# Cross attention on one core: other places in the queue for the large loads, key parts in transfers of 24 rows, split maxima sent one step earlier

## The chip, the cores and the metric

One core of a Trainium2 chip (trn2) runs one launch. The metric is the device time of that launch in microseconds (us), lower is better. Engines: PE (matmul), ACT (ScalarE), DVE (VectorE), POOL (GpSimd), SP (SyncE, which only issues DMAs). Matmuls run at a clock that the chip grants: 2.4 GHz (shown as 1.00) or 1.2 GHz (0.50).

## The reference, cut to what matters

Cross attention of 16 batch rows with 256 queries each over 1601 keys (16 heads of 8 dimensions), then a local-attention block of 6 layers that the change does not touch:

```
scores = einsum('bhqd,bhkd->bhqk', q, k) / sqrt(8)
scores = where(mask, -1e9, scores)
attn   = softmax(scores)                     # over 1601 keys, fp32
x      = x + tanh(g) * (einsum('bhqk,bhkd->bhqd', attn, v) @ w_o + b_o)
```

## The kernel before, in words

`cross_phase` handles one batch row per iteration, and three rows are in flight: `cur` (its softmax and its products), `nxt` (its keys, queries and values are projected, its operands loaded) and `prev` (its output). An iteration has 4 groups, q = 0 to 3, of 4 heads each, and a group has KT = 13 steps, one per tile of 128 keys. Below, "step (q, kt)" is step kt of group q.

In every step PE makes the scores of one key tile into the two banks `b_e` (line 756 adds the mask, line 760 multiplies keys and queries); ACT takes exp of each into `eT` (line 442, two instructions a step); PE multiplies the exps of the step before with the values (line 662). A bank of `b_e` is written again only when its exp of the step before is done, so PE and ACT hold each other to within one step. Beside that PE makes other scores `b_s` (line 742), two groups ahead, from which DVE takes the maxima (line 515), and the small matmuls of `nxt` and `prev` (the list in `uses`).

**Operands.** q and k are split into three bfloat16 parts. They go out to DRAM (`k_scr`, line 303; `q_scr`, line 313) and come back in another layout: `k_op[q]`, one tensor for each group, rows 24a + 8c + d (a, c = 0 to 2, d = 0 to 7) by `load_k` in nine transfers of 8 rows of 12808 bytes (line 265); `q_op`, for all groups, in nine transfers of 8 rows (line 322). The negated maximum of each query goes into three further rows of `q_op`: PE transposes it at step TURN = 7, DVE negates it (line 528), POOL splits it in three with five small instructions (`max_parts`, lines 363 to 372, semaphore `mp_ready`), and ACT sends the parts in three small transfers (line 486) at step 10 of the group before the one that reads them; PE waits for them (`mrow_in`) at step 0 of that group, ahead of line 756.

**Order on SP's queue in one iteration:** `xa`, `xb` (lines 284, 290), `x1_scr`, `xn_scr` (293, 296), `k_scr`, then `load_k` 0 (waits until group 0 of `cur` is done with `k_op[0]`), `q_scr`, `q_op` (waits for the last but one row only), `load_k` 1 (waits for group 1), the next row's context `ctxT` (line 255) and masks (258, 259), `load_k` 2 (group 2), `load_k` 3 (group 3). SP takes them strictly in turn.

**At step (0, 10)** ACT also makes a part of the keys (`kp`, line 461) ahead of the small transfers. At step (0, 7) it made the first one (line 457), on which POOL's subtraction (line 379) waits; `max_parts` is queued behind that.

Of the kernel before, what the change touches and what calls it, by code (L numbers as in the profile page):

```python
# [48 lines left out]
HX, DK = 16, 8  # L49
MROW = 9 * DK  # L50
KEYS = 1601
KT = -(-KEYS // P)
# [42 lines left out]
def cross_phase(nc, x1_scr, xn_scr, ident, identb, ins, NB):  # L95
# [6 lines left out]
    with ExitStack() as ctx:  # L102
        def sb(name, shape, dt=F32):
            return ctx.enter_context(nc.sbuf_tensor(name, shape, dt))

        def sem(name):
            return ctx.enter_context(nc.semaphore(name))
# [10 lines left out]
        k_op = [sb(f"k_op{i}", [P, 4, KEYS], BF16) for i in range(4)]  # L118
# [28 lines left out]
        k_scr = nc.dram_tensor("k_scr", [2, 3, P, KEYS], BF16, kind="Internal").ap()  # L147
# [21 lines left out]
        s = {n: sem(n) for n in (*per, *dma_per)}  # L169
        per.update(dma_per)  # L170
        kop_in = [sem(f"kop_in{i}") for i in range(4)]
        KOP = 9 * 16
        pool_passed = sem("pool_passed_x")
        dve_passed = sem("dve_passed_x")
        start_in = sem("start_in")
# [19 lines left out]
        def count(name, b, c, back=0):  # L195

            return (b - back + AHEAD) * per[name] + c

        def max_index(q):

            return 1 if q == 3 else q + 2

        def start_ahead(eng, names):
            for name in names:
                eng.sem_inc(s[name], AHEAD * per[name])
# [40 lines left out]
        @block.sync  # L246
        def _(sp):
            start_ahead(sp, dma_per)
            for dst, src in ((w_sb[:, :], ins["x_w"]), (vec[:, :], ins["x_vec"]), (bv[:, :], ins["bv"]),
                             ):  # L250
                sp.dma_start(dst, src).then_inc(start_in, 16)

            def load_ctx(b):

                sp.dma_start(ctxT[:, :], ins["ctx"][:, b, :]).then_inc(s["ctx_in"], 16)

            def load_masks(b):
                sp.dma_start(m8[:, :, :], ins["mask_q"][b]).then_inc(s["m8_in"], 16)
                sp.dma_start(mt8[:, :, :], ins["mask_k"][b]).then_inc(s["mt8_in"], 16)

            def load_k(b, p, q):
                for a in range(3):
                    for c in range(3):
                        r = 24 * a + 8 * c
                        sp.dma_start(k_op[q][r:r + DK, :, :],
                                     k_scr[p, c].rearrange("(d h) k -> d h k", d=DK)[:, 4 * q:4 * q + 4, :]
                                     ).then_inc(kop_in[q], 16)

            load_ctx(0)
            load_masks(0)
            sp.wait_ge(set_pool, N_SETX)
            for i in range(4):
                sp.dma_start(k_op[i][MROW:MROW + 3, :, :], onesr[:, :].unsqueeze(1).to_broadcast([3, 4, KEYS])
                             ).then_inc(ones_in, 16)

            def iteration(cur, nxt, prev, base):
                if nxt:
                    b = nxt[0]  # L280

                    sp.wait_ge(start_in, 48)
                    sp.wait_ge(s["lcq_ready"], count("lcq_ready", b, 1, back=1))
                    sp.dma_start(xa[:, :], ins["xin"][:, b, :]).then_inc(s["xa_in"], 16)
                if prev:
                    b = prev[0]

                    sp.wait_ge(start_in, 48)
                    sp.wait_ge(s["y1_ready"], count("y1_ready", b, 1, back=1))
                    sp.dma_start(xb[:, :], ins["xin"][:, b, :]).then_inc(s["xb_in"], 16)  # L290
                    sp.wait_ge(start_in, 48)
                    sp.wait_ge(s["y1_ready"], count("y1_ready", b, 1))
                    sp.dma_start(x1_scr[:, b, :], y1[:, :]).then_inc(s["x1_kept"], 16)
                    sp.wait_ge(start_in, 48)
                    sp.wait_ge(s["xn_ready"], count("xn_ready", b, 1))
                    sp.dma_start(xn_scr[:, b, :], xn[:, :]).then_inc(s["xn_kept"], 16)
                if nxt:
                    b, p = nxt
                    sp.wait_ge(start_in, 48)
                    sp.wait_ge(s["klo_ready"], count("klo_ready", b, 1))  # L300

                    for c in range(3):
                        sp.dma_start(k_scr[p, c], kp[:, c, :]).then_inc(s["kscr_in"], 16)
                    sp.wait_ge(start_in, 48)
                    sp.wait_ge(s["kscr_in"], count("kscr_in", b, 48))

                    sp.wait_ge(start_in, 48)
                    sp.wait_ge(s["e_done"], count("e_done", b, 2 * KT, back=1))
                    load_k(b, p, 0)
                    sp.wait_ge(start_in, 48)  # L310
                    sp.wait_ge(s["qlo_ready"], count("qlo_ready", b, 1))
                    for c in range(3):
                        sp.dma_start(q_scr[p, c], qp[:, c, :]).then_inc(s["qscr_in"], 16)
                    sp.wait_ge(start_in, 48)
                    sp.wait_ge(s["qscr_in"], count("qscr_in", b, 48))

                    sp.wait_ge(start_in, 48)
                    sp.wait_ge(s["e_done"], count("e_done", b, 8 * KT, back=2))
                    for a in range(3):
                        for c in range(3):  # L320
                            r = 24 * a + 8 * c
                            sp.dma_start(q_op[r:r + DK, p, :, :], q_scr[p, a].rearrange("(d h) q -> d h q", d=DK)
                                         ).then_inc(s["qop_in"], 16)
                    sp.wait_ge(start_in, 48)
                    sp.wait_ge(s["e_done"], count("e_done", b, 4 * KT, back=1))
                    load_k(b, p, 1)
                if nxt:
                    b, p = nxt

                    sp.wait_ge(start_in, 48)  # L330
                    sp.wait_ge(s["vx_ready"], count("vx_ready", b, 4))
                    load_ctx(b + 1)
                    sp.wait_ge(start_in, 48)
                    sp.wait_ge(s["mq_ready"], count("mq_ready", b, 1))
                    sp.wait_ge(s["mk_ready"], count("mk_ready", b, 1))
                    load_masks(b + 1)
                if nxt:
                    b, p = nxt
                    for q in (2, 3):
                        sp.wait_ge(start_in, 48)  # L340
                        sp.wait_ge(s["e_done"], count("e_done", b, 2 * KT * (q + 1), back=1))
                        load_k(b, p, q)

            rows(sp, iteration)

            sp.wait_ge(s["ctx_in"], count("ctx_in", NB, 16))
            sp.wait_ge(s["x1_kept"], count("x1_kept", NB, 0))
            sp.wait_ge(s["xn_kept"], count("xn_kept", NB, 0))
            sp.wait_ge(s["m8_in"], count("m8_in", NB, 16))
            sp.wait_ge(s["mt8_in"], count("mt8_in", NB, 16))  # L350
# [61 lines left out]
        def _(act):  # L412
# [17 lines left out]
            def iteration(cur, nxt, prev, base):  # L430
                where = uses(cur, nxt, prev)
                for q in range(4):
                    for kt in range(KT):
                        if cur:
                            b, p = cur
# [9 lines left out]
                        for i, (*when, kind, j) in enumerate(where):  # L445
                            if tuple(when) == at and kind == "k":
                                b = nxt[0]
# [5 lines left out]
                        if nxt and at == (0, 7):  # L453
                            b = nxt[0]
# [3 lines left out]
                        if nxt and at == (0, 10):  # L458
                            b = nxt[0]
                            act.wait_ge(s["kres_ready"], count("kres_ready", b, 1))  # L460
                            nc.scalar.activation(kp[:, 1, :], kf[:, :], ACT.Copy).then_inc(s["kmid_ready"], 1)
                        if nxt and at == (1, 2):
                            b = nxt[0]
# [3 lines left out]
                        if nxt and at == (1, 4):  # L467
                            b = nxt[0]
# [3 lines left out]
                            rstd("q", nxt, 0)  # L472
                        if prev and at == (1, 0):
                            rstd("y", prev, 1)
                        if kt == 10:

                            item = (cur, q + 1) if q < 3 else (nxt, 0)
                            if item[0]:
                                (b, p), sq = item
                                m = max_index(q)  # L480
                                bm = b
                                act.wait_ge(s["mp_ready"], count("mp_ready", bm, m))

                                act.wait_ge(s["e_done"], count("e_done", bm, 8 * KT, back=2))
                                for c in range(3):
                                    act.dma_start(q_op[MROW + c:MROW + c + 1, p, 4 * sq:4 * sq + 4, :], mp[:, c, :]
                                                  ).then_inc(s["mrow_in"], 16)
            rows(act, iteration)

        @block.vector  # L490
# [150 lines left out]
        def _(pe):  # L641
# [6 lines left out]
            def iteration(cur, nxt, prev, base):  # L648
# [78 lines left out]
                for q in range(4):  # L727
                    for kt in range(KT):
                        row, sq, at = group_at(cur, nxt, q, kt)
                        if row:  # L730
                            b, p = row
                            if at == 0:
                                pe.wait_ge(kop_in[sq], b * KOP + KOP)
                                pe.wait_ge(s["qop_in"], count("qop_in", b, 9 * 16))
# [941 lines left out]
```

## Time and profile before

| | |
|---|---|
| median of 3 runs | 5901.35 us (5883.94 to 5910.17) |
| profiled execution: its time | 5897.66 us |
| its span | 5895.9 us |
| mean granted clock | 0.978 |
| cross attention lies at | about 0 to 2090 us of the span |

The profiled execution is 3.7 us under the median and 1.8 us over its own span. Times of rows are us from the span's start. "xN" is a count, and a bracket at the end of a line gives the idle time just before it and what ended it.

### The profile page before, as it was taken

The numbers are of one execution on the slowest core, as the hardware profiler recorded it, in microseconds if no ns is written. First come the engines' busy times: TensorE is split into PE (matmuls) and PEld (weight loads), VectorE is DVE, ScalarE is ACT, GpSimd is POOL, SyncE is SP. The second block draws the span as 40 slices with busy tenths as digits, with TensorE's granted clock in tenths as the row PEclk, the third lists the DMA queues.
The fourth block names the chain that finished last, engine by engine and source line by source line (L and its number), as shares of the span: only waits on it lengthen the run. The fifth ranks groups of instructions, "written<-read, shape, count | busy, mean of one in ns | idle before, by whom it ended". The sixth has DMA issues, their size and how long they took to land.

```text
span 5895.9 us, 158903 instructions
## 1 busy us (share of the span) xinstructions
PE 5562.7 (94%) x51848; PEld 3300.2 (56%) x51848; DVE 3635.5 (62%) x8009; ACT 4014.3 (68%) x10790; POOL 2651.8 (45%) x2284
## 2 busy tenths in 40 slices
PE   5999999999999969999999999999999999999997
PEld 2444444444444436666666666666666666666665
DVE  3666676666666546666666666666666666666664
ACT  2555555445555547787888778888888788878885
POOL 2211121111122045666566666565665556666663
PEclk9999999999999989999999999999999999999999
DMA  3343333333323233333333333333333333333332
GB/s 79 64 74 61 63 56 66 67 69 63 63 56 72 39 113 91 98 95 113 106 96 96 107 103 102 99 104 103 98 98 109 103 98 96 98 118 94 98 98 87
DMA packets 147237, 518.47 MB, mean 88 GB/s; under 512 B 32188, under 2 KB 48444, under 8 KB 127980
## 3 DMA queue, kind: packets, MB, share of 16 engines
q1 hardware_dynamic: 144876, 507.59, 33.3%
q8 instruction: 455, 7.45, 0.6%
q14 instruction: 370, 3.03, 0.2%
q10 hardware_dynamic: 1536, 0.40, 0.0%
HBM read 224.98 MB, written 30.68 MB: 43 GB/s over the span
## 4 chain that ended last, share of the span: by engine, by line
PE 45%; ACT 11%; issue 5%; DVE 2%; POOL 0%; ACTq 0%; DMA 0%; DVEq 0%; SPq 0%; POOLq 0%
PE b_qk L1448 9%; PE b_c L1489 6%; PE b_pt L1387 5%; PE b_o L1407 5%; ACT probs L1150 4%; PE b_sc L1375 4%; PE b_qk L1459 4%; PE b_nv L1423 3%; PE b_sc L1366 2%; PE b_c L1519 2%; ACT L1189 2%; ACT L79 2%; PE b_nv L1519 1%; ACT ln_n L1115 1%; ACT gg L1189 1%
## 5 line engine op out<-in xcount | busy, mean ns | idle before, releaser
L442 ACT ACTIVATE eT<-b_e 128x512 f32<-128x512 f32 (+1 forms) x1664 | 907.9, 594 | 977.2 <-PE b_e L760 971.9
L1150 ACT ACTIVATE probs<-b_sc,nb,rq 128x96 f32<-128x96 f32 (+1 forms) x3072 | 1322.8, 448 | 10.6 <-DVE nb L1283 9.4
L515 DVE CUSTOM_DVE_ANT_0 junk<-b_s,mq 128x1024 bf16<-128x1024 f32 (+1 forms) x1024 | 1000.2, 991 | 446.3 <-PE b_s L742 423.2
L1074 POOL TENSOR_TENSOR probs<-probs,rsums 128x512 f32<-128x512 f32 (+1 forms) x768 | 716.7, 933 | 694.4 <-DVE rsums L1219 693.0
L1274 DVE TENSOR_REDUCE b_sc<-b_sc 128x4 f32<-128x512 f32 (+1 forms) x768 | 486.1, 633 | 818.3 <-PE b_sc L1375 815.5
L1137 ACT ACTIVATE probsT<-b_pt 128x512 f32<-128x512 f32 x768 | 455.8, 593 | 559.3 <-PE b_pt L1387 558.4
L1448 PE MATMUL b_qk<-xs,weights 128*128 128x256 f32 x3072 | 745.9, 386 | 54.0 <-ACT sq L1164 32.4
L756 PE MATMUL b_e<-mk,identb 128*128 128x512 bf16 (+1 forms) x1664 | 656.9, 395 | 53.2 <-DMA q_op<-mp 41.8
L760 PE MATMUL b_e<-q_op,k_op 75*128 75x256 bf16 (+1 forms) x3328 | 660.7, 280 | 0.0
L1150 ACT ACTIVATION_READ_ACCUMULATOR probs<-b_sc,nb,rq 128x1 f32 x3072 | 643.1, 209 | 0.0
L1448 PEld LDWEIGHTS b_qk<-xs,weights 128*128 128x128 f32 x3072 | 558.7, 192 | 142.1 <-ACT sq L1164 44.7
L1407 PEld LDWEIGHTS b_o<-probsT,v 128*64 128x64 f32 x9216 | 372.0, 137 | 441.5 <-issue 304.3
L1253 DVE TENSOR_TENSOR rot_s<-b_qk,rot_tab 128x512 f32<-128x512 f32 x768 | 526.0, 685 | 123.2 <-PE b_qk L1448 117.7
L1043 POOL TENSOR_TENSOR kT<-kT,rot_p 128x1024 f32<-128x1024 f32 x192 | 454.6, 2368 | 310.8 <-DMA rot_p<-rot_s 283.1
L742 PE MATMUL b_s<-k_op,q_op 72*128 72x512 bf16 (+1 forms) x2048 | 517.6, 351 | 39.4 <-issue 25.9
L662 PE MATMUL b_pv<-eT,vx 128*9 128x256 f32 x6656 | 533.5, 393 | 3.9 <-ACT eT L442 3.9
L1407 PE MATMUL b_o<-probsT,v 128*64 128x64 f32 (+1 forms) x9216 | 516.2, 247 | 19.0 <-DVE oT L1211 7.2
L1164 ACT ACTIVATE sq<-b_qk 128x512 f32<-128x512 f32 x768 | 447.8, 598 | 121.6 <-DVE kT L1259 62.8
L1387 PE MATMUL b_pt<-ident,probs 128*128 128x128 f32 x3072 | 505.6, 287 | 0.3 <-POOL probs L1074 0.3
L1051 POOL TENSOR_TENSOR kT<-kT,rkb 128x1024 f32<-128x1024 f32 x192 | 452.1, 2355 | 100.3 <-DMA rkb<-rk_scr 100.1
L760 PEld LDWEIGHTS b_e<-q_op,k_op 75*128 75x128 bf16 (+1 forms) x3328 | 340.4, 102 | 274.0 <-issue 36.2
L1043 POOL TENSOR_TENSOR qT<-qT,rot_p 128x1024 f32<-128x1024 f32 x192 | 453.4, 2362 | 66.6 <-DMA rot_p<-rot_s 44.7
(133 smaller groups left out, 8347.1 us busy)
## 6 DMA issues: line engine op xcount, KB each, us to landing
rot_p<-rot_s SPq DMA_DIRECT2D x768, 256.0 KB, 2.4
rkb<-rk_scr SPq DMA_DIRECT2D x192, 512.0 KB, 6.3
k_op<-k_scr SPq DMA_DIRECT2D x576, 100.1 KB
v<-v SPq DMA_DIRECT2D x192, 256.0 KB, 3.5
k_scr<-kp SPq DMA_DIRECT2D x48, 400.2 KB, 3.4
weights<-in_ffn_w SPq DMA_DIRECT2D x27, 512.0 KB, 4.8
ctxT<-in_ctx SPq DMA_DIRECT2D x17, 800.5 KB, 20.1
q_op<-q_scr SPq DMA_DIRECT2D x144, 64.0 KB
```

The source lines that it names most:

```text
L442: nc.scalar.activation(eT[0:n, g % 2, i * 512:(i + 1) * 512], b_e[i][0:n, :], ACT.Exp).then_inc(s["e_ready"], 1)
L515: nc.vector.tensor_tensor_reduce(junk[:, half, 0:n], b_s[u % 2][:, 0:n], mq[:, p, qt, half * 1024:half * 1024 + n], 1.0, LOWEST, ALU.add, ...
L662: last = nc.tensor.matmul(b_pv[32 * h:32 * h + DK + 1, 0:S], vx[0:n, p, kt, 4 * q + h, :], eT[0:n, g % 2, h * S:(h + 1) * S], start=(kt == ...
L756: nc.tensor.matmul(b_e[i][0:n, :], identb[0:n, 0:n], mk[0:n, p, kt, :].unsqueeze(1).to_broadcast([n, 2, S]), start=True, stop=False, skip_ ...
L760: last = nc.tensor.matmul(b_e[i][0:n, j * S:(j + 1) * S], k_op[q][0:MROW + 3, 2 * i + j, kt * P:kt * P + n], q_op[0:MROW + 3, p, 4 * q + 2 ...
L1043: nc.gpsimd.tensor_tensor(dst, dst, rot_p[:, i % 2, :].rearrange("p (j t) -> p j t", j=4), ALU.add).then_inc(s["sum_ready"], 1)
L1074: nc.gpsimd.tensor_tensor(pu, pu, rsums[:, u % 2, :].unsqueeze(2).to_broadcast([P, 4, w]), ALU.mult).then_inc(s["pn_ready"], 1)
L1150: last = nc.scalar.activation(probs[:, t, k % 2, 2 * e + h, c0:P], b_sc[:, 512 * e + h * w:512 * e + (h + 1) * w], ACT.Exp, bias=nb[:, k % ...
L1253: nc.vector.tensor_tensor(per_block(rot_s[:, q % 2, 512 * (i % 2):512 * (i % 2 + 1)]), per_block(src), rot_tab[:, tab + 1, :].unsqueeze(1) ...
L1387: last = nc.tensor.transpose(b_pt[:, i * P:(i + 1) * P], probs[:, t, u % 2, i, :], ident[:, :])
L1407: last = nc.tensor.matmul(b_o[r, o0 + q0:o0 + q1], v[:, p, tile, vc], probsT[:, u % 2, c + q0:c + q1], start=True, stop=True, skip_group_c ...
L1448: last = nc.tensor.matmul(b_qk[:, 512 * (i % 2) + x * S:512 * (i % 2) + (x + 1) * S], weights[:, c0:c0 + P], xs[:, p, :], start=True, stop ...
```

## The change

Line numbers are those of the kernel before. `load_k` makes three transfers of 24 rows in place of nine of 8 (the same bytes: all nine rows' blocks of `k_scr[p]` are read once per a). On SP's queue `q_op` now waits for group 1 of `cur`, as `load_k` 1 behind it does; `load_k` 2 stands ahead of the context and the masks; `load_k` 3 keeps the last place. ACT sends the split maxima at step 9.

```diff
-        KOP = 9 * 16
+        KOP = 3 * 16
...
             def load_k(b, p, q):
+                src = k_scr[p].rearrange("c (d h) k -> (c d) h k", d=DK)[:, 4 * q:4 * q + 4, :]
                 for a in range(3):
-                    for c in range(3):
-                        r = 24 * a + 8 * c
-                        sp.dma_start(k_op[q][r:r + DK, :, :],
-                                     k_scr[p, c].rearrange("(d h) k -> d h k", d=DK)[:, 4 * q:4 * q + 4, :]
-                                     ).then_inc(kop_in[q], 16)
+                    sp.dma_start(k_op[q][24 * a:24 * a + 24, :, :], src).then_inc(kop_in[q], 16)
...
-                    sp.wait_ge(s["e_done"], count("e_done", b, 8 * KT, back=2))
+                    sp.wait_ge(s["e_done"], count("e_done", b, 4 * KT, back=1))
                     for a in range(3):
                         for c in range(3):
                             r = 24 * a + 8 * c
                             sp.dma_start(q_op[r:r + DK, p, :, :], q_scr[p, a].rearrange("(d h) q -> d h q", d=DK)
                                          ).then_inc(s["qop_in"], 16)
-                    sp.wait_ge(start_in, 48)
-                    sp.wait_ge(s["e_done"], count("e_done", b, 4 * KT, back=1))
                     load_k(b, p, 1)
                 if nxt:
                     b, p = nxt
-
+                    sp.wait_ge(start_in, 48)
+                    sp.wait_ge(s["e_done"], count("e_done", b, 6 * KT, back=1))
+                    load_k(b, p, 2)
                     sp.wait_ge(start_in, 48)
                     sp.wait_ge(s["vx_ready"], count("vx_ready", b, 4))
                     load_ctx(b + 1)
...
                     load_masks(b + 1)
-                if nxt:
-                    b, p = nxt
-                    for q in (2, 3):
-                        sp.wait_ge(start_in, 48)
-                        sp.wait_ge(s["e_done"], count("e_done", b, 2 * KT * (q + 1), back=1))
-                        load_k(b, p, q)
+                    sp.wait_ge(start_in, 48)
+                    sp.wait_ge(s["e_done"], count("e_done", b, 8 * KT, back=1))
+                    load_k(b, p, 3)
...
-                        if kt == 10:
+                        if kt == 9:
```

## Rows read from the trace of the kernel before

**Rows 1.** The page: the span, and PE's line (busy us, share, instructions)

```profile
span 5895.9 us, 158903 instructions
...
PE 5562.7 (94%) x51848; PEld 3300.2 (56%) x51848; DVE 3635.5 (62%) x8009; ACT 4014.3 (68%) x10790; POOL 2651.8 (45%) x2284
```

**Rows 2.** Waits of PE, 226 to 1976 us: us in total, times, longest us

```profile
PE b_e L756 <- DMA q_op<-mp: 41.8, 21, 4.1
```

**Rows 3.** Timeline of PE: start, us, what, idle time before

```profile
666.01 0.39 PE L756 MATMUL b_e<-mk,identb 128*128 128x512 bf16 x1 [2.54 <-DMA q_op<-mp]
...
945.09 0.61 PE L756 MATMUL b_e<-mk,identb 128*128 128x512 bf16 x1 [3.61 <-DMA q_op<-mp]
945.49 0.63 PE L760 MATMUL b_e<-q_op,k_op 75*128 75x256 bf16 x2
```

**Rows 4.** Windows: length, busy us (x) by engine, granted clock, DMA share, GB/s

```profile
226.00:1976.00 1750.00, 1691.88 (x12869) 751.77 (x12866) 1144.70 (x2281) 893.21 (x1622) 330.58 (x364) 0.95 0.36 65
...
290.00:305.00 15.00, 15.00 (x72) 5.11 (x70) 5.66 (x11) 5.21 (x9) 0.00 (x0) 0.54 0.75 108
...
1915.00:1931.00 16.00, 13.80 (x67) 4.70 (x68) 5.19 (x11) 4.78 (x8) 0.00 (x0) 0.57 0.68 96
```

**Rows 5.** Timeline of SP's queue, one iteration (group 1 from 634 us)

```profile
649.78 2.99 SPq L265 DMA_DIRECT2D k_op<-k_scr  x9
...
665.43 3.00 SPq L322 DMA_DIRECT2D q_op<-q_scr  x9
...
671.80 0.37 SPq L255 DMA_DIRECT2D ctxT<-in_ctx  x1
```

**Rows 6.** Timeline of ACT's queue in the same iteration

```profile
658.30 1.81 ACTq L486 DMA_DIRECT2D q_op<-mp  x3
```

**Rows 7.** Windows of the same iteration, columns as in rows 4

```profile
660.00:663.00 3.00, 3.00 (x29) 1.32 (x27) 2.66 (x6) 1.84 (x4) 0.00 (x0) 1.00 0.47 65
...
666.00:672.00 6.00, 5.99 (x31) 1.93 (x32) 1.66 (x3) 2.29 (x4) 0.00 (x0) 0.57 0.51 82
```

**Rows 8.** Timeline of PE: first use of the new q_op and k_op[0]

```profile
684.17 0.61 PE L742 MATMUL b_s<-k_op,q_op 72*128 72x512 bf16 x2
```

**Rows 9.** Timeline of all engines around step (0, 10)

```profile
627.14 1.08 ACT L442 ACTIVATE eT<-b_e 128x512 f32<-128x512 f32 x2 [1.22 <-PE b_e L760]
627.16 0.44 POOL L372 CAST mp<-mres 4x256 bf16<-4x256 f32 x1 [0.17 <-POOL mres L369]
...
627.74 0.60 ACTq L486 DMA_DIRECT2D q_op<-mp  x1
...
628.11 1.54 ACT L461 ACTIVATE kp<-kf 128x1601 bf16<-128x1601 f32 x1
...
629.17 0.38 PE L756 MATMUL b_e<-mk,identb 128*128 128x512 bf16 x1
```

**Rows 10.** The same place in the first iteration

```profile
137.36 1.82 ACTq L486 DMA_DIRECT2D q_op<-mp  x3
...
139.29 1.08 ACT L442 ACTIVATE eT<-b_e 128x512 f32<-128x512 f32 x2 [2.01 <-issue]
...
139.94 0.41 PE L756 MATMUL b_e<-mk,identb 65*65 65x512 bf16 x1 [0.94 <-ACT eT L442]
```

**Rows 11.** Timeline around step (2, 10): last split, and PE at step 11

```profile
689.81 0.39 POOL L372 CAST mp<-mres 4x256 bf16<-4x256 f32 x1 [0.17 <-POOL mres L369]
...
692.58 0.38 PE L756 MATMUL b_e<-mk,identb 128*128 128x512 bf16 x1
```

**Rows 12.** Timeline of PE: the first group of the first row

```profile
106.49 0.59 PE L756 MATMUL b_e<-mk,identb 128*128 128x512 bf16 x1 [8.76 <-issue]
```

**Rows 13.** Timeline of PE at the loop's jump, and a window after the second

```profile
471.90 0.42 PE L742 MATMUL b_s<-k_op,q_op 72*128 72x512 bf16 x2 [1.35 <-issue]
...
977.84 0.42 PE L742 MATMUL b_s<-k_op,q_op 72*128 72x512 bf16 x2 [1.01 <-issue]
...
977.00:986.00 9.00, 8.16 (x51) 3.50 (x52) 5.22 (x11) 3.26 (x6) 0.00 (x0) 1.00 0.63 104
```

## The prediction, made before the changed kernel ran

> **What bounds the kernel now.** I read the page first: PE is busy for 94% of the span [rows 1], so the kernel is as long as PE's work, PE's idle time and PE's slow time. The change touches only cross attention, so I asked for PE's waits over the fourteen regular iterations. One line stands out: 41.8 us in 21 waits, all for the small transfers that carry the split maxima into q_op [rows 2]. The timeline shows two kinds. At step 0 of group 2 PE stands for 2.54 us until 666.01 us. At step 0 of group 3 it stands for 3.61 us until 945.09 us, and the matmul behind that takes 0.63 us where 0.38 is usual: it runs at the low clock [rows 3]. So I read the clock next. It averages 0.95 over 1750 us, and a stretch at the low level loses half its length: (1 - 0.95) x 1750 = 87 us [rows 4]. There are 19 low stretches; 15 of them (the first and the last are in rows 4: (1 - 0.54) x 15 = 6.9 us, (1 - 0.57) x 16 = 6.9 us) follow or overlap such a wait. The other four follow PE's 1.0 to 1.35 us of idle time at the loop's jump, 3.4 us each [rows 13]. That leaves 87 - 14 = 73 us; in some of the 15 the low stretch begins while PE still stands, which costs nothing twice, so I count 62.
>
> **Why the small transfers are late.** SP asks for k_op[0] at 649.78 us [rows 5]; ACT sends the small ones at 658.30 [rows 6]. At 660 to 663 us the DMA engines are busy by 0.47, about 8 of 16, at 65 GB/s: that is k_op[0] alone, 0.92 MB [rows 7]. PE would have gone on at 666.01 - 2.54 = 663.47, and it got the rows at 666.0, 7.7 us after the first was sent. In group 0 the same transfers take about 3 us. They come in just behind the large load, as if they stood in one line with it. The Trainium skill ("DMA: Bandwidth & Descriptors", Queues, rings and completion order) says that an engine takes turns between the queues of SP and ACT packet by packet. By that rule the small ones would pass after a turn each, sending them earlier would help as it stands, and shortening the large load would be worth little (rival D). The trace speaks for one line, and I go by it. The group 3 waits have the same look, behind context and masks (asked for at 671.80 [rows 5]).
>
> **The change, part by part.**
>
> *Large loads moved (group 3 waits).* Context and masks leave group 2 and are asked for behind k_op[2], at the start of group 3. What is left ahead of group 3's small transfers is q_op and k_op[1]: 0.59 MB and 0.92 MB at 65 to 82 GB/s [rows 7] are some 21 us, and a group is about 26 us long, with the sending at 18 us. The waits of group 3 go: 15.5 us of the 41.8. Next late could be group 0's small transfers, now behind k_op[2], context and masks: 2.55 MB. At the 96 to 108 GB/s that the mixed stretches reach [rows 4] that is 24 to 26 us, and the group is 26 us long. At its end the rate is higher, as no k_op is left, and I take this as just hidden. It is the thinnest cover of the change.
>
> *q_op behind group 1.* It is asked for when group 1 ends, about where it stands now (665.43, [rows 5]), and no longer just behind k_op[0]. The first matmul that reads it starts at 684.17 [rows 8], 18 us after group 2's start (about 14 at full clock), and 0.59 MB at 82 GB/s take 7 us: hidden, cost nothing. That clears the line behind k_op[0].
>
> *Key parts in 24 rows (group 2 waits).* k_op[0] stays where it was, as it waits for k_scr. So group 2's waits, 26.3 us, go only if it comes sooner. No row shows a 24-row transfer. One end: the rate is that of the reading and stays, 13 us or, with more engines in each other's way, somewhat over; nothing is gained and the waits grow by as much. The other: it goes like the fastest mixed window, or faster, 108 GB/s [rows 4], 8.5 us. Eight engines moved 65 to 85 GB/s. More rows can use more engines, and I take about 9 us, nearer to the mixed windows, where more than 8 engines work too. What is needed: the last row in by 663.5 - 1.1, which is 12.6 us after the asking. At 9 us there are 3 us to spare. The Trainium skill (same page, "Why a DMA increments its semaphore by 16 and not by 1") has a transfer use the largest number of engines up to 16 that divides its slowest dimension: 8 for 8 rows, 12 for 24. It agrees with the 0.47. By it I estimate 13 x 8 / 12 = 9 us. The skill's "SBUF — State Buffer" (the DMA port swizzle) gives 8 adjacent partitions two ports and 24 of them six, which would be faster still. SP issues 3 in place of 9 transfers (2.99 us for nine [rows 5]); nothing waits for that time.
>
> *The start.* PE stands for 8.76 us before row 0 [rows 12] with the same loads in flight. With shorter loads the small transfers are through in time: -8.7. The other end is 0.
>
> *Sending at step 9.* Three issues hold ACT's instruction stream for 1.8 us, and the exps behind them wait. In group 0 the split is ready only at 627.60 (627.16 + 0.44), and step 10's exps began at 627.14 [rows 9]. Now these come behind the wait and the issues. The first iteration shows the size: issued from 137.36, next exp at 139.29, and PE stands 0.94 us for it [rows 10]. So step 10's first exp starts at about 627.7 + 1.9 = 629.6 and ends at 630.2 (0.6 for one). PE's line 756 of step 11 stood at 629.17 and now at 630.3: 1.1 us late. Then ACT still owes the second exp and the key part (1.54 us [rows 9]), which makes step 12 later by another 0.2. Cost 1.3 us x 14 = 18 us, and 3 us more in the first iteration. For groups 3 and 0 (sent at steps (2, 9), (3, 9)) the split is ready at 689.81 + 0.39 = 690.2; issues until 692.1, exp 692.3 to 692.9, against PE's 692.58 [rows 11]: 0.5 us each, 2 x 14 x 0.5 = 14. For group 2 step 10 is longer and nothing is lost. Sum +35; the ends are +15 (the issues hide behind exps already handed to ACT) and +50. What it buys: the small transfers are off 2 us sooner, and nothing that I count needs that.
>
> *The clock.* 1.1 us of standing is a size at which the clock sometimes falls. Of ten stretches of 1.0 to 1.4 us in this trace six were followed by the low level (1.35 at 471.90 was, 1.01 at 977.84 was not: its window stays at 1.00 [rows 13]). I take 9 of 14, at 2.6 us each: +24. Ends: 0, and 14 at 4.5 us, +63.
>
> **Sum**, against the profiled execution of 5897.7 us: -41.8 - 62 - 8.7 + 35 + 24 = -53, so 5845. The median of the runs is 3.7 us above that execution: 5848 in the median. The case's own range, with the ends combined, is 5815 to 5890.
>
> **Rivals.**
>
> *A: k_op[0] is not faster (slower than before).* The place is the read of k_scr: if the rate is held by the source, or 12 engines share what 8 had, k_op[0] still needs 13 us and group 2's waits stay with their clock. It decides from 12.6 us after the asking. Gone are then only group 3's 15.5 us and 19 us of clock; -34.5 + 35 + 24 = +24: 5925. For it: the rate was 65 in one window and 82 in another at the same number of engines, so something other than their number sets it. Against it: context moved beside k_op at 108.
>
> *B: the early sending costs nothing*, since ACT has spare time in most steps: -53 - 59 = -112, 5789. Against it: PE's 0.94 us in the first iteration is the same thing.
>
> *C: the clock falls at each new standing, and for longer*: 14 x 4.5 = 63 in place of 24: 5887. For it: it fell six times of ten. Against it: four times it did not.
>
> *D: k_op[0] is not faster, but the queues take turns.* Then each small transfer waits for about one large packet, whatever is behind, and sending from 656.1 in place of 658.3 makes each wait 2.2 us shorter, where the mean of the 21 is 2.0: nearly all go, and only the start stays as it is: -53 + 8.7 = -44, 5857. Against it: at 658.3 five more us of k_op[0] were to come, and the rows landed behind all of it. This is the skill's rule of turns, cited above.
>
> **How the numbers follow.** My forecast 0.60, A 0.16, B 0.09, C 0.11, D 0.04. What a measurement of this kernel can tell from no change is about 0.5%, 29 us: faster means below 5872, slower above 5931. Faster: 0.51 of my 0.60, B and most of D, 0.63. Slower: about half of A and what could come late at group 0, 0.10. Within: the rest, 0.27. The range 5812 to 5926 takes in my case, C, D and A up to its middle; B and half of A, 0.17, are left out.
>
> **What would show it.** Right: PE's wait for q_op<-mp nearly gone from groups 2 and 3; k_op[0] landed (DMA share back to 0) within 10 us of its issue; a new PE wait for eT of 1.0 to 1.3 us at step (0, 11), 14 times, and 0.4 to 0.6 us at step 11 of groups 2 and 3; a mean clock over the regular iterations above 0.97; row 0 starting at 98 us. Wrong: waits of 2 us or more at group 2's start (A); no wait for eT (B); a wait at group 0's start, which would mean that context and masks came too late there; a wait at L742 for q_op.

## The result, and the profile after

| | before | after |
|---|---|---|
| median | 5892.65 us (5880.83 to 5910.17, 4 runs) | 5813.08 us (5809.61 to 5816.44, 4 runs) |
| profiled execution | 5897.66 us | 5809.61 us |
| its span | 5895.9 us | 5807.8 us |
| mean granted clock | 0.978 | 0.990 |

The ratio is 0.9863, with a 95% interval of 0.9833 to 0.9892: the kernel is 1.4% faster. The forecast was faster too, but by 53 us, 5848 in the median; the medians lie 80 us apart, and the two profiled executions, against which the forecast was summed, 88 us. The page of the kernel after has PE busy for 56 us less than in [rows 1], for the same 51848 matmuls:

```profile
span 5807.8 us, 158510 instructions
...
PE 5506.6 (95%) x51848; PEld 3280.0 (56%) x51848; DVE 3645.4 (63%) x8009; ACT 4008.7 (69%) x10790; POOL 2651.7 (46%) x2284
```

The same matmuls cost less time only at a higher clock. Where in the span did that happen? The first and the last matmul of line 756 of before, now line 750, bound cross attention. Kernel before, then kernel after, from the view of the tile `identb` (ns of the shortest, the median and the longest, then first and last start):

```profile
L756 PE MATMUL b_e<-mk,identb x1664: 378/379/634, 106.5 to 2077.2; 128*128 128x512 bf16 x171, 65*65 65x512 bf16 x14
```

```profile
L750 PE MATMUL b_e<-mk,identb x1664: 378/379/637, 91.2 to 1993.2; 128*128 128x512 bf16 x171, 65*65 65x512 bf16 x14
```

Cross attention ends 84 us sooner (2077.2 against 1993.2), of which 15 us are there when the first row begins. That is all but 4 of the 88 us. What lies behind it is the same code in all kernels, with low clock of its own (90.7 us of low stretches before, 75.1 after). From the last matmul of this line to the end it took 3815 to 3830 us in the ten profiled executions of this document. So one profile can't tell less than about 15 us of the whole time from nothing; the end of cross attention is the surer measure.

**The waits.** PE's waits over the regular iterations, kernel after, 226 to 1880 us (us in total, times, longest):

```profile
PE b_e L750 <- ACT eT L436: 19.1, 34, 1.2
PE b_s L736 <- issue: 5.2, 6, 1.1
```

The line of [rows 2], 41.8 us for `q_op<-mp` (39.5 of it before 1880 us), is gone, and a new one is there, for `eT`. Its members of over 0.9 us are fourteen, one per iteration, at step (0, 11). The other line is the loop's jump.

**The clock.** The kernel after in four windows (length, busy us (x) by engine, granted clock, DMA share, GB/s, as in [rows 4]):

```profile
226.00:1880.00 1654.00, 1618.66 (x12773) 727.41 (x12772) 1146.40 (x2264) 881.99 (x1612) 330.44 (x364) 1.00 0.28 68
628.00:632.00 4.00, 4.00 (x38) 1.74 (x35) 2.66 (x6) 2.22 (x5) 2.09 (x4) 1.00 0.82 192
634.00:636.00 2.00, 2.00 (x19) 0.82 (x17) 0.96 (x4) 1.08 (x2) 1.53 (x1) 1.00 0.01 2
124.00:142.00 18.00, 16.98 (x76) 6.55 (x76) 5.85 (x13) 8.09 (x14) 5.89 (x2) 0.55 0.42 121
```

The mean clock of the regular iterations went from 0.95 to 1.00. Stretch by stretch, over the regular iterations of each kernel (before: to 1976 us), the low clock held for 171 us in 19 stretches before and for 13.7 us in 2 after, both at the loop's jump. The last line is the first row, which had no low stretch before and now has one of 17.1 us.

**The key load.** SP's queue of the kernel after, one iteration:

```profile
626.36 1.12 SPq L264 DMA_DIRECT2D k_op<-k_scr  x3
627.58 1.39 SPq L310 DMA_DIRECT2D q_scr<-qp  x3
639.15 2.98 SPq L319 DMA_DIRECT2D q_op<-q_scr  x9
642.18 24.08 SPq L264 DMA_DIRECT2D k_op<-k_scr  x6
666.53 0.37 SPq L255 DMA_DIRECT2D ctxT<-in_ctx  x1
```

`k_op[0]` is asked for at 626.36, and the windows above give the rest: the DMA engines are busy by 0.82 at 192 GB/s from 628 to 632 and by 0.01 at 634. In [rows 7] the same bytes went at 0.47 and 65 GB/s. (The 192 hold the store of `q_scr`, asked for at 627.58, 0.19 MB beside the 0.9 MB of `k_op[0]`.) From the issue to the last semaphore count of the load it is 7.5 to 7.9 us in all batch rows, where it was 12.9 to 15.7. So PE finds its operands at the start of group 2, and nothing stands ahead of line 750:

```profile
639.87 0.38 PE L750 MATMUL b_e<-mk,identb 128*128 128x512 bf16 x1
```

**Step 9.** The kernel after around steps (0, 10) and (0, 11), all engines:

```profile
602.27 0.44 POOL L366 CAST mp<-mres 4x256 bf16<-4x256 f32 x1 [0.17 <-POOL mres L363]
...
602.74 1.82 ACTq L480 DMA_DIRECT2D q_op<-mp  x3
...
604.76 1.09 ACT L436 ACTIVATE eT<-b_e 128x512 f32<-128x512 f32 x2 [3.73 <-issue]
...
605.41 0.39 PE L750 MATMUL b_e<-mk,identb 128*128 128x512 bf16 x1 [0.97 <-ACT eT L436]
```

POOL ends the split at 602.71, ACT issues until 604.56, and the exps of step 10, queued behind that, start at 604.76, after 3.73 us in which ACT did nothing else. PE gets its bank back 0.97 us late.

### The profile page after: what moved, and what is told of

It is laid out like the page before. It is cut to its first block, busy times and chain, and to the rows that moved or that the text cites. A ratio compares the mean times of both kernels' runs of the same rounds, so it can differ in the third digit from the quotient of the medians.

```text
span 5807.8 us, 158510 instructions
## 1 busy us (share of the span) xinstructions
PE 5506.6 (95%) x51848; PEld 3280.0 (56%) x51848; DVE 3645.4 (63%) x8009; ACT 4008.7 (69%) x10790; POOL 2651.7 (46%) x2284
## 4 chain that ended last, share of the span: by engine, by line
PE 45%; ACT 12%; issue 5%; DVE 2%; DMA 1%; POOL 1%; ACTq 0%; SPq 0%; DVEq 0%; POOLq 0%
PE b_qk L1442 9%; PE b_c L1483 6%; PE b_pt L1381 5%; PE b_o L1401 5%; ACT probs L1144 4%; PE b_sc L1369 4%; PE b_qk L1453 4%; PE b_nv L1417 3%; PE b_sc L1360 2%; PE b_c L1513 2%; ACT L1183 2%; ACT L79 2%; PE b_nv L1513 1%; ACT ln_n L1109 1%; ACT gg L1183 1%
## 5 line engine op out<-in xcount | busy, mean ns | idle before, releaser
L750 PE MATMUL b_e<-mk,identb 128*128 128x512 bf16 (+1 forms) x1664 | 639.8, 385 | 27.0 <-ACT eT L436 25.5
L754 PE MATMUL b_e<-q_op,k_op 75*128 75x256 bf16 (+1 forms) x3328 | 642.9, 274 | 0.0
L736 PE MATMUL b_s<-k_op,q_op 72*128 72x512 bf16 (+1 forms) x2048 | 505.0, 343 | 31.8 <-issue 17.2
L656 PE MATMUL b_pv<-eT,vx 128*9 128x256 f32 x6656 | 519.6, 384 | 3.9 <-ACT eT L436 3.9
```

Of the source, the lines that this page charges most:

```text
L656: last = nc.tensor.matmul(b_pv[32 * h:32 * h + DK + 1, 0:S], vx[0:n, p, kt, 4 * q + h, :], eT[0:n, g % 2, h * S:(h + 1) * S], start=(kt == ...
L750: nc.tensor.matmul(b_e[i][0:n, :], identb[0:n, 0:n], mk[0:n, p, kt, :].unsqueeze(1).to_broadcast([n, 2, S]), start=True, stop=False, skip_ ...
L754: last = nc.tensor.matmul(b_e[i][0:n, j * S:(j + 1) * S], k_op[q][0:MROW + 3, 2 * i + j, kt * P:kt * P + n], q_op[0:MROW + 3, p, 4 * q + 2 ...
```

## The experiments

Eight kernels; the kernel before had a median of 5905 us beside them, against 5893 beside the change. The last two columns are PE's waits from 226 to 1880 us, for the small transfers (`q_op<-mp`, 39.5 us in the kernel before) and for `eT`. The window is the same for all, so it holds fewer rows of a slower kernel.

| | median us | ratio to before (95%) | for q_op<-mp | for eT |
|---|---|---|---|---|
| undo_step9 | 5777.27 | 0.9781 (0.9765 to 0.9796) | none | none |
| only_rows24 | 5788.74 | 0.9805 (0.979 to 0.982) | 3.9 us | none |
| only_order | 5879.37 | 0.9958 (0.9946 to 0.997) | 29.4 us | none |
| only_step9 | 5933.05 | 1.0038 (1.0024 to 1.0053) | 34.5 us | 18.0 us |
| stride9 | 5820.76 | 0.9861 (0.9837 to 0.9885) | none | 19.1 us |
| step8 | 6147.54 | 1.0406 (1.0375 to 1.0436) | none | 117.7 us |
| step9_not_group0 | 5792.59 | 0.9806 (0.9785 to 0.9826) | none | 4.8 us |
| spread3_step10 | 5779.5 | 0.9786 (0.9767 to 0.9806) | none | none |

They are the lines of `b_e` in that view; "none" is where it has no such line.

### The change without step 9

```diff
-                        if kt == 9:
+                        if kt == 10:
```

> The changed kernel with the small transfers sent at step 10 again. Theory 1 (sending at step 9 only costs): PE's 14 waits for eT of 1.0 to 1.2 us at step (0, 11) vanish, a group 0 takes 34.5 us in place of 35.8, groups 2 and 3 lose 0.2 and 0.5 us, in all 2.1 us a row and 3 us in the first: 32 us less than the changed kernel, about 5781 us. The slack of the small transfers (3.5 to 5 us in the changed kernel) shrinks by 2 us and stays above 0, so no wait for q_op<-mp returns. Rival (the earlier step is what hides them): waits for q_op<-mp of 0.5 us and more return at groups 1 to 3, and the time is 5813 us or more.

Measured: 0.9781, the fastest of all. That step 9 costs time is shown; how much, less sharply. The two ratios differ by 0.82% of the kernel, 48 us, but the interval of the change's ratio is 0.3% to each side, and the kernel before was itself 12 us slower beside the second. The two medians lie 36 us apart, and cross attention ends 36.7 us sooner in the profile. PE's longest line of waits (226 to 1880 us) is now the loop's jump, and cross attention ends at 1956.5:

```profile
PE b_s L736 <- issue: 8.3, 6, 1.7
```

```profile
L750 PE MATMUL b_e<-mk,identb x1664: 378/380/634, 92.2 to 1956.5; 128*128 128x512 bf16 x171, 65*65 65x512 bf16 x14
```

Group by group, from the first matmul of line 750 of a group to that of the next, in the iterations without low clock:

| us | group 0 | 1 | 2 | 3 |
|---|---|---|---|---|
| step 9 (after) | 35.8 | 29.6 | 26.0 | 26.95 |
| step 10 (undo_step9) | 34.53 | 29.34 | 25.62 | 26.48 |
| difference | 1.27 | 0.26 | 0.38 | 0.47 |

2.4 us in each of 14 rows is 33 us. The first row lasts 127.0 us with step 9 and 116.7 without, another 10. The sum is 43. In the profile 37 are left of it: this execution had low clock at four of its loop's jumps, the change's at two, some 7 us. And the small transfers need no head start: sent at step 10 they are there 1.5 to 4.6 us before group 0, 3.3 before group 1, 2.1 before group 2 and 1.9 before group 3.

### The 24-row transfers alone

The kernel before, with the change's `load_k` and `KOP = 3 * 16`, the queue's order and step 10 as they were.

```diff
-        KOP = 9 * 16
+        KOP = 3 * 16
...
-                    for c in range(3):
-                        r = 24 * a + 8 * c
...
+                    sp.dma_start(k_op[q][24 * a:24 * a + 24, :, :], src).then_inc(kop_in[q], 16)
```

> The kernel before with the 24-row transfers alone, old order, step 10. Theory 1 (the length of the key loads is the cause of both kinds of wait): k_op[0] lands 7.6 us after its issue in place of 15, group 2's waits vanish, and as k_op[1] is some 5 us shorter too, the masks are through before group 3's small transfers are needed, so those waits vanish as well: 5893 - 42 - 75 (clock) - 16 (start) + some clock at the loop's jump = 5765 to 5785 us. Theory 2 (the places of context and masks matter on their own): group 3's waits stay, 10 to 16 us and their low clock, and the time is 5795 to 5815 us.

Measured: 0.9805. This one edit brings more than the whole change; it takes the waits for `q_op<-mp` (226 to 1880 us) from 39.5 us to one line of 3.9, and row 0 starts at 92.1 us. What is left are seven waits at group 2, in row 1 and every second row after, as here:

```profile
PE b_e L753 <- DMA q_op<-mp: 3.9, 7, 1.0
```

```profile
861.93 0.39 PE L753 MATMUL b_e<-mk,identb 128*128 128x512 bf16 x1 [0.95 <-DMA q_op<-mp]
```

In the old order `q_op` is asked for about 8 us behind `k_op[0]`, within 1.1 us of the small transfers, and these take 4.5 to 6.0 us there where they take 2.9 with nothing in flight. None of the seven waits, at most 0.95 us, was followed by the low clock.

### The new order alone

The change with nine 8-row transfers and with step 10.

```diff
-                    sp.dma_start(k_op[q][24 * a:24 * a + 24, :, :], src).then_inc(kop_in[q], 16)
+                    for c in range(3):
+                        r = 24 * a + 8 * c
+                        sp.dma_start(k_op[q][r:r + DK, :, :], ...).then_inc(kop_in[q], 16)
...
-                        if kt == 9:
+                        if kt == 10:
```

> The kernel before with the new order of the loads alone: nine transfers of 8 rows, step 10. Both theories: k_op[0] still needs 13 to 15 us, group 2's waits stay (26 us of standing and some 40 us of low clock), group 3's go (15 us and some 20 us of clock): about 5857 us. Rival (the place of q_op behind k_op[0] was part of it): group 2's waits shrink too, below 5840 us. Group 0's small transfers now stand behind k_op[2], context and masks: a new wait there would show that cover as too thin.

Measured: 0.9958, 26 us under the kernel before beside it, where 36 were expected. Waits of PE, and the window 226 to 1880 us:

```profile
PE b_e L753 <- DMA q_op<-mp: 29.4, 14, 3.2
```

```profile
226.00:1880.00 1654.00, 1608.77 (x12297) 718.82 (x12295) 1099.82 (x2187) 856.84 (x1556) 320.06 (x348) 0.96 0.35 65
```

Group 3's waits go, all but one of 0.76 us, and group 2's stay, with their clock, at 0.96: the low stretches of the regular iterations fall only from 171 to 147 us, which is 12 us of time, not the 20 expected. That is rival A's machine with step 9 taken out. With both edits (undo_step9) the gain is 2.19%; the parts alone are 0.42% and 1.95%, in sum a little more than both together. Both clear the same waits of group 3, which would explain that; the difference, 0.18%, is not clear of the intervals.

### Step 9 alone

The kernel before with `kt == 9`.

```diff
-                        if kt == 10:
+                        if kt == 9:
```

> The kernel before with the sending at step 9 alone. Theory 1 (one line behind the large loads): the waits for q_op<-mp at groups 2 and 3 keep their size, since the rows land behind the large load whenever they are sent, and 32 us of waits for eT and late steps come on top, with 0 to 24 us of clock: 5925 to 5945 us. Rival (the queues take turns): each wait for q_op<-mp shrinks by 2 us, nearly all go with 60 us of low clock: below 5850 us.

Measured: 1.0038, slower. Waits of PE, 226 to 1880 us:

```profile
PE b_e L756 <- DMA q_op<-mp: 34.5, 15, 3.5
PE b_e L756 <- ACT eT L442: 18.0, 32, 1.2
```

SP's and ACT's queue and PE at one group 2:

```profile
660.81 2.98 SPq L265 DMA_DIRECT2D k_op<-k_scr  x9
```

```profile
666.33 1.81 ACTq L486 DMA_DIRECT2D q_op<-mp  x3
```

```profile
676.61 0.39 PE L756 MATMUL b_e<-mk,identb 128*128 128x512 bf16 x1 [2.77 <-DMA q_op<-mp]
```

The small transfers are off a step sooner and land no sooner: 7.8 to 10.9 us under way at group 2, where it was 5.6 to 8.1. They land only when the key load of 660.81 is through; the store `q_scr`, which SP asks for behind it at 663.89, lies ahead of them too. This settles rival D, whose waits would have gone; they stay at 2.3 us each (34.5 / 15). The Trainium skill ("DMA: Bandwidth & Descriptors", Queues, rings and completion order) has the engines take turns between the two queues packet by packet, and puts some 9 to 17 descriptors in a packet. A turn after each large row, as rival D reads it, is not what the trace shows. But `k_op[0]` is 72 rows on about 8 engines, nine for each, so whether the rule fails here or its packet is as long as the whole load stays open.

### What makes the key load fast: engines or partitions

Nine transfers of 8 rows, as before, but to rows j, j + 9, j + 18, ... in place of eight adjacent ones, for `k_op` and `q_op` both; the rest is the change, step 9 too.

```diff
-                    sp.dma_start(k_op[q][24 * a:24 * a + 24, :, :], src).then_inc(kop_in[q], 16)
+                    for c in range(3):
+                        sp.dma_start(k_op[q][3 * a + c:MROW:9, :, :], ...).then_inc(kop_in[q], 16)
...
-                            sp.dma_start(q_op[r:r + DK, p, :, :], ...
+                            sp.dma_start(q_op[3 * a + c:MROW:9, p, :, :], ...
```

> The changed kernel (new order, step 9) with nine transfers of 8 rows again, but each writes rows j, j + 9, ... of k_op and q_op in place of 8 adjacent ones (q_op's rows in the same order, so the products are the same). Theory P (what limits a load is how many groups of adjacent partitions it writes at once): the same eight engines now move 12808 bytes in about 0.5 us, a key load lands 6 to 7 us after its issue and q_op in 4 to 5 us in place of 10.7, no wait for q_op<-mp, ratio to the kernel before 0.985 to 0.988. Theory E (each engine has its rate, and 24 rows only brought more engines): 12 to 14 us for a key load as in the kernel before, the waits at group 2's start are back, ratio 1.00.

Measured: 0.9861, as the change itself. It has no wait for `q_op<-mp`. The window of `k_op[0]`:

```profile
627.00:630.00 3.00, 3.00 (x25) 1.45 (x24) 1.67 (x6) 1.24 (x3) 1.73 (x4) 1.00 0.45 145
```

The DMA share is 0.45, where [rows 7] have 0.47 for 8 adjacent rows, and the rate is 145 GB/s in place of 65. No other load is in flight in this window (`q_scr` is asked for at 630.82). So 8 engines are not the limit at 65 GB/s; where the rows lie is. `k_op[0]` takes 8.4 to 9.4 us in most rows (11.0 and 11.4 in two), not the 6 to 7 expected, and `q_op` 7.5 to 8.7 where it took 10.6 to 10.9 in the change. 24 adjacent rows, with a share of 0.82, are faster still at 7.5 to 7.9 us. Whether that is the number of engines is not shown: SP needs 5.80 us to issue the nine spread transfers and 1.12 for the three of 24 rows, so the last of the nine starts late, and no run separates the two. The Trainium skill ("SBUF — State Buffer", the DMA port swizzle) has 8 adjacent partitions share two ports and 24 six: the two rates agree in direction with it.

Spread rows on top of 24-row transfers, with step 10:

```diff
-                    sp.dma_start(k_op[q][24 * a:24 * a + 24, :, :], src).then_inc(kop_in[q], 16)
+                    sp.dma_start(k_op[q][a:MROW:3, :, :], src).then_inc(kop_in[q], 16)
...
-                            r = 24 * a + 8 * c
-                            sp.dma_start(q_op[r:r + DK, p, :, :], ...
+                            r = 24 * c + a
+                            sp.dma_start(q_op[r:r + 22:3, p, :, :], ...
```

> The version meant to be best: new order, step 10, and three key transfers of 24 rows that write every third row of 72, q_op's 8-row transfers every third row of 24 (rows of both in the same order). Theory P: key loads land in 5 us, q_op in 6 us; as no small transfer waits any more, only the start gains, 3 to 8 us on the version with step 10 alone (ratio 0.9781): 0.9765 to 0.978. Theory E: no faster load, 0.978.

Measured: 0.9786, no different from undo_step9. `k_op[0]` takes 7.0 to 7.9 us, hardly less than 24 adjacent rows and not the 5 expected, and `q_op` 7.6 to 9.0. Row 0 starts at 88.9 in place of 92.2 us; but no wait was left to take away.

### How far early sending can be pushed, and where the clock falls

```diff
-                        if kt == 9:
+                        if kt == 8:
```

> The changed kernel with the small transfers sent one more step earlier, at step 8: this makes ACT's wait for POOL's split longer. Expected: at step (0, 8) ACT waits some 3 to 5 us, and PE's 14 waits for eT of 1.0 to 1.2 us become waits of 3 us and more; at the other groups the split is not ready either and 2 us are lost each. About 14 x (3 + 3 x 2) = 120 us more. Theory C1 (the clock did not fall in the changed kernel because a wait of 1.0 to 1.2 us is just too short at these places): now it falls at nearly every group 0, 14 times, mean clock over the regular rows 0.95 or lower. Theory C2 (the clock falls only where the matmuls before the wait are sparse too, as at the loop's jump): it stays at 0.99.

Measured: 1.0406. Waits and window of 226 to 1880 us:

```profile
PE b_e L750 <- ACT eT L436: 117.7, 47, 4.0
```

```profile
226.00:1880.00 1654.00, 1515.21 (x10755) 652.04 (x10756) 986.71 (x1909) 754.35 (x1360) 278.97 (x302) 0.90 0.24 57
```

Here ACT stands for the split in every group, and PE for ACT. It costs some 330 us on the change's median, where 120 were expected: the low clock, at 0.90, came on top. This kernel also helps to tell at which waits the clock falls:

| wait of PE, at | length, us | followed by the low level |
|---|---|---|
| after, step (0, 11) | 0.97 to 1.23 | 0 of 14 |
| only_step9, step (0, 11) | 0.96 to 1.24 | 0 of 14 |
| step8, (1, 10) | 1.22 to 1.40 | 0 of 15 |
| step8, (0, 11) | 1.43 to 1.97 | 3 of 10, those from 1.78 up |
| step8, (2, 10) and (3, 10) | 2.21 to 2.57 | 22 of 30 |
| step8, (0, 10) | 3.71 to 5.64 | 15 of 15 |
| before, start of groups 2 and 3, from 1.00 up | 1.00 to 4.10 | 15 of 18, not 1.00, 1.08 and 1.81 |
| only_order, start of group 2, from 1 us up | 1.36 to 3.21 | 13 of 13 |
| only_step9, start of group 2 | 1.38 to 3.48 | 12 of 13, the 1.38 not |
| loop's jump, all kernels but step8 | 0.91 to 1.66 | 33 of 47; the longest that was not, 1.39 |

Two waits of about the same size, with the windows behind them, first only_order at the start of group 2, then step8 at step (1, 10):

```profile
1400.20 0.39 PE L753 MATMUL b_e<-mk,identb 128*128 128x512 bf16 x1 [1.45 <-DMA q_op<-mp]
```

```profile
1401.00:1412.00 11.00, 11.00 (x57) 3.67 (x58) 4.42 (x9) 4.09 (x8) 0.00 (x0) 0.53 0.53 75
```

```profile
1007.70 0.39 PE L750 MATMUL b_e<-mk,identb 128*128 128x512 bf16 x1 [1.37 <-ACT eT L436]
```

```profile
1008.00:1017.00 9.00, 9.00 (x78) 4.00 (x80) 5.22 (x11) 4.79 (x10) 0.07 (x1) 1.00 0.19 35
```

One costs 11 us at 0.53, the other nothing. Just ahead of a group's start, and of the loop's jump, PE has worked on the last tile, which has 65 keys and not 128; ahead of step (1, 10) it worked on full tiles. That this is the reason is a reading of the table; no run changed it alone. It is no sharp rule either: in the kernel before, 1.81 us at a start of group 2 was followed by no low stretch.

```profile
1797.48 0.39 PE L756 MATMUL b_e<-mk,identb 128*128 128x512 bf16 x1 [1.81 <-DMA q_op<-mp]
```

```profile
1797.00:1808.00 11.00, 10.52 (x88) 4.61 (x88) 6.00 (x12) 5.50 (x11) 0.00 (x0) 1.00 0.66 96
```

### Step 9 for all groups but the first

```diff
-                        if kt == 9:
+                        if kt == (10 if q == 0 else 9):
```

> The changed kernel, with the sending at step 10 in group 0 and at step 9 in groups 1 to 3. Theory (the cost of step 9 lies in group 0, where POOL's split is late): group 0 takes 34.5 us again, PE's waits for eT are gone there, groups 2 and 3 keep their +0.4 and +0.5 us and group 1 its +0.3 or nothing. Saved against the changed kernel: 14 x 1.3 = 18 us and 10 us in the first row (3.4 us of standing and the 17 us of low clock behind it), so the ratio to the kernel before is 0.9863 - 0.0047 = 0.981 to 0.982. Rival (the three issues cost the same everywhere): 0.984 or more.

Measured: 0.9806. Group 0 is back at 34.53 us, the first row at 117.6, and what is left of the waits is

```profile
PE b_e L750 <- ACT eT L436: 4.8, 21, 0.4
```

So the larger part of the cost hangs on the send in group 0, where the split is ready after step 9's exps: 30 of the 36.7 us by which cross attention ended sooner (1963.2 here), 21 of 36 in the medians. The intervals of this kernel and of undo_step9 overlap (0.9785 to 0.9826, 0.9765 to 0.9796), so the rest isn't clear of noise in the times; groups 2 and 3 still last 26.0 and 26.95 us.

## Why the prediction was right and wrong

**Right: the mechanism and the waits.** The small transfers stood in one line behind `k_op[0]`; with a shorter load they are in time, and the 41.8 us [rows 2] are gone. The forecast needed `k_op[0]` within 12.6 us of its issue and took 9; it was 7.5 to 7.9. Group 0 stays covered behind `k_op[2]`, context and masks, and `q_op` comes 3.3 to 3.6 us ahead of its first use: no wait at either. Rivals A and D fell by one measurement each, 192 GB/s after and the waits that stayed in only_step9.

**Right: the price of step 9 per row.** Forecast 32 us in the 14 rows (1.3 at group 0, nothing at group 1, 0.5 at groups 2 and 3), measured 1.27, 0.26, 0.38 and 0.47: 33 us. Rival B, that it costs nothing, fell.

**Wrong: the clock term of step 9.** "I take 9 of 14, at 2.6 us each: +24." It was 0 of 14. This step failed: it counted the falls of the trace of before by the length of the wait alone, and the waits that it counted stood at the loop's jump and at the starts of groups. Amid full tiles, waits of 0.96 to 1.40 us were followed by the low level 0 times in 43 (14 + 14 + 15). Why those are spared is open. Rival C stood on the same count.

**Mis-sized: the start, -8.7, measured -15.3** (106.5 to 91.2 us). The step took only PE's 8.76 us of idle time [rows 12]. The shorter `k_op[0]` also lets the first scores (`b_s`), which read it, start 6 to 7 us sooner, and they lie ahead of the first row.

**Mis-sized: the recovered clock, -62, measured -75.** In the regular iterations PE was at work for 163 us of the 171 us of low stretches before, and for 13.7 us after: half of the difference is 75. The forecast took 11 us off for low clock that fell into PE's standing; it was half of 171 - 163, 4 us. And 7 of the 75 are no effect of the edits as far as the runs show: two low stretches at the loop's jump where there were four, but again four in undo_step9 and in only_rows24.

**Mis-sized: the first iteration, +3, measured +10, and the last, left out, +4.** The first one's first step 9 holds PE for 3.42 us, and the clock is low for 17.1 us behind it (the window 124 to 142 above):

```profile
125.02 0.61 PE L750 MATMUL b_e<-mk,identb 128*128 128x512 bf16 x1 [3.42 <-ACT eT L436]
```

The last row took 102.1 us before and 105.8 after. The sum with the measured terms is -41.8 - 75 - 15.3 + 33 + 10 + 4 = -85, against -84 at the end of cross attention. Of the 31 us or so by which the forecast's -53 fell short, the clock of step 9 is 24, the recovered clock 13 and the start 7; the first and the last row take back 7 and 4, the price of step 9 one. So the number was missed mainly by the step that failed, and for a smaller part by luck at the loop's jump.

**The change as a whole.** It is three edits, one of them harmful. The order alone brings 0.42%, 24-row transfers alone 1.95%, both 2.19%, and step 9 gives back 0.6 to 0.8 of that. The forecast did say that nothing it counted needed step 9.

## What to carry to other kernels

When an engine waits for a small transfer, look at what is in flight from the other queues: a large load issued just ahead can hold it, and shortening that load helps where sending earlier does not. A load's time depends on which partitions it writes at once; more rows per transfer halved it here, and rows spread over the partitions took a third off. A DMA issue on a computing engine is paid in that engine's stream, so put it where its input is already there.

## What the runs showed of the hardware that was not expected

- The same share of the DMA engines (0.47 and 0.45) moved 65 GB/s into 8 adjacent rows and 145 GB/s into 8 rows nine apart. 24 adjacent rows went at 192 GB/s and a share of 0.82, with the stores of `q_scr` beside them.
- SP needs longer to issue transfers to rows nine apart: 5.80 us for nine, against 2.98 for nine adjacent ones. No wait of PE came of it here, but it is most of the 8.4 us that the load takes at least:

```profile
624.91 5.80 SPq L264 DMA_DIRECT2D k_op<-k_scr  x9
```

- PE's clock fell after all 13 waits of 1.36 us and more at the start of group 2 in only_order, and after none of the 43 of 0.96 to 1.40 us amid full tiles. So a wait's price depends on where it stands, and moving a wait is not neutral. The 1.81 us in the kernel before, behind which the clock stayed up, show that its length and place do not settle it alone.
